# Masking attention's future keys: zeroed in the exponentials on VectorE, or added to the scores on TensorE

## The reference, cut to what matters

```python
scores = jnp.einsum('bhqd,bhkd->bhqk', q, k) / math.sqrt(hd)
causal = jnp.triu(jnp.ones((S, S), dtype=bool), k=1)
scores = jnp.where(causal[None, None], -jnp.inf, scores)
attn = jax.nn.softmax(scores, axis=-1)
attn_out = jnp.einsum('bhqk,bhkd->bhqd', attn, v)
```

## Time and profile before

| | us |
|---|---|
| median of 3 runs | 1922.88 (1922.86 to 1925.65) |
| the profiled execution | 1917.86 |
| its span, first to last instruction | 1916.0 |
| TensorE busy | 1823.9 (95%) |
| VectorE busy | 1022.4 (53%) |
| ScalarE busy | 744.5 (39%) |
| GpSimd busy | 659.2 (34%) |

### The profile page before, as it was taken

The page is one execution under the profiler, slowest core; times in us unless marked ns, Lnnn a source line. Parts: engine busy times, 40 slices in busy tenths (PEclk is TensorE's granted clock), DMA queues, the critical chain, the costliest instruction groups (busy, mean ns, idle before and its releaser), DMA issues.

```text
span 1916.0 us, 29823 instructions
## 1 busy us (share of the span) xinstructions
PE 1823.9 (95%) x11604; PEld 1361.1 (71%) x11604; DVE 1022.4 (53%) x2155; ACT 744.5 (39%) x1542; POOL 659.2 (34%) x831
## 2 busy tenths in 40 slices
PE   4886899999999999999999999999999999999888
PEld 2575746986489845997479855997479864898457
DVE  5675365635565365645655365644656365653531
ACT  5842345133542346133452245223451335322441
POOL 2242333423353233523343232632343232532110
PEclk9897999999999999999999999999999999999789
DMA  4001000000000000000000000000000000000000
GB/s 151 11 23 45 12 2 11 1 1 23 12 1 1 12 12 12 1 1 23 12 1 1 11 13 12 1 1 22 12 1 1 1 23 1 1 1 11 1 1 11
DMA packets 20202, 23.78 MB, mean 12 GB/s; under 512 B 960, under 2 KB 18784, under 8 KB 20064
## 3 DMA queue, kind: packets, MB, share of 16 engines
q1 hardware_dynamic: 19728, 20.83, 3.4%
q0 software_dynamic: 336, 1.05, 0.2%
HBM read 17.68 MB, written 4.19 MB: 11 GB/s over the span
## 4 chain that ended last, share of the span: by engine, by line
PE 84%; DVE 4%; ACT 2%; issue 2%; POOL 1%; POOLq 0%; DVEq 0%; ACTq 0%
PE ring L1457 17%; PE ring L1442 17%; PE ring L1497 8%; PE ring L1418 7%; PE ring L1428 6%; PE ring L1594 5%; PE attn_out L1614 4%; PE ring L1552 3%; PE ring L1574 3%; PE ring L1577 2%; PE ring L1410 2%; PE ring L1597 2%; PE ring L1466 2%; PE ring L1528 1%; PE ring L1530 1%
## 5 line engine op out<-in xcount | busy, mean ns | idle before, releaser
L1203 DVE TENSOR_REDUCE maxes<-ring 128x2 f32<-128x768 f32 (+7 forms) x292 | 198.0, 735 | 91.8 <-PE ring L1577 90.9
L1127 DVE COPY_PREDICATED scores_t<-masks,ring 128x512 f32<-128x512 uint16 x224 | 160.7, 731 | 104.2 <-issue 95.3
L670 POOL TENSOR_TENSOR rstd<-mean_var,eps_and_power 128x2 f32<-128x2 f32 x96 | 19.3, 201 | 493.1 <-DVE mean_var L1050 493.1
L1497 PEld LDWEIGHTS ring<-big 128*128 128x128 f32 x1536 | 180.4, 194 | 10.8 <-issue 4.9
L1497 PE MATMUL ring<-big 128*128 128x128 f32 x1536 | 182.7, 277 | 4.4 <-POOL big L721 3.1
L721 POOL TENSOR_TENSOR big<-big,decay_blocks 128x256 f32<-128x256 f32 x192 | 141.0, 747 | 111.3 <-issue 86.5
L1457 PE MATMUL ring<-w_down,big 128*128 128x256 f32 x768 | 172.4, 380 | 0.0
L1457 PEld LDWEIGHTS ring<-w_down,big 128*128 128x128 f32 x768 | 144.5, 190 | 18.5
L693 POOL TENSOR_TENSOR mix<-mix,z_t 128x512 f32<-128x512 f32 x80 | 86.2, 1104 | 152.4 <-DVE mix L1097 152.4
L1594 PE MATMUL ring<-big 32*128 32x512 f32 (+3 forms) x1024 | 123.9, 481 | 3.4 <-issue 1.7
L894 ACT ACTIVATE big<-ring,up_bias 128x256 f32<-128x256 f32 x192 | 80.5, 470 | 99.0 <-PE ring L1442 99.0
(11 more groups left out here) (192 smaller groups left out, 3483.2 us busy)
## 6 DMA issues: line engine op xcount, KB each, us to landing
x_in<-in_x SPq DMA_DIRECT2D x8, 512.0 KB, 3.8
out<-x_z_xb SPq DMA_DIRECT2D x8, 512.0 KB, 2.9
delta<-in_x SPq DMA_DIRECT2D x7, 512.0 KB, 3.8
w_mlp<-in_wm SPq DMA_DIRECT2D x2, 1024.0 KB, 7.0
w_mlp<-in_w_exp_t SPq DMA_DIRECT2D x1, 1028.0 KB, 14.1
v_ones<-in_w_con SPq DMA_DIRECT2D x1, 1024.0 KB, 9.9
w_k<-in_wk SPq DMA_DIRECT2D x1, 512.0 KB, 7.4
rope<-in_rope POOLq DMA_DIRECT2D x1, 512.0 KB, 6.6
```

Source lines behind the costliest of these rows:

```text
L1127: ins = nc.vector.copy_predicated(scores[:, h, :, :], lmask[:, lv, :].bitcast(U16).unsqueeze(1) .to_broadcast([P, NT, P]), chunks)
L1203: nc.vector.tensor_reduce(maxes[:, t % 2, qt, 32 * gs[0] + row:32 * gs[-1] + row + 1:32], banks[:, first:last, lo:hi], AX_X, ALU.max).then ...
L1497: ins = mm(ps[:, tok], kg[:, h, tok], q[:, h, tok], start=True, stop=True)
```

## The change

The mask product of `s_exp` goes. The score products are no longer followed by an accumulating product, so each carries its own stop flag, and the last part's product signals that the bank is full. A new step `hide(t, rnd)`, only on VectorE, waits until the four exponentials of the round are written and then overwrites with zero those that belong to future keys, with one predicated copy of 128x512 (4 heads x 128 queries) in rounds a and c and two in round b. Its mask is the tile `future_t` read as 16-bit words; its data is one zero element, broadcast. `V(t, rnd)` waits for `hide(t, rnd)` in place of the four exponentials. The list places hide(t,a) behind S(t+1,a), hide(t,b) behind S(t+1,b) and hide(t,c) behind S(t+1,c). The masks of S stay.

```diff
@@ attention_steps
-        o += fill[0] + [("E", t, "b")] + fill[1] + [("V", t, "a")]
+        o += [("hide", t, "a")] + fill[0] + [("E", t, "b")] + fill[1] + [("V", t, "a")]
         o += [("S", t + 1, "b")] if ahead else []
+        o += [("hide", t, "b")]
         o += [("roundq", 3, "all")] if t == 1 else []
         o += [("V", t, "b")] + fill[2] + [("E", t, "c")] if ahead else fill[2] + [("E", t, "c"), ("V", t, "b")]
         o += [("S", t + 1, "c")] if ahead else []
-        o += fill[3] + [("V", t, "c")]
+        o += [("hide", t, "c")] + fill[3] + [("V", t, "c")]
@@ VectorE
+            def future_hidden(t, part):
+                dve.wait_ge(*after(pt_ready, exp_count(t, part, HG - 1)))
+                if b == 0 and t == 0 and part == "a":
+                    dve.wait_ge(*loaded(masks_in))
+                    dve.wait_ge(consts.h, N_CONSTS)
+                for at in (0, P) if part == "b" else (0,):
+                    ins = nc.vector.copy_predicated(pt[part][:, :, at:at + P], future_t.bitcast(U16).unsqueeze(1)
+                                                    .to_broadcast([P, HG, P]),
+                                                    zt[:, 0, 0:1].unsqueeze(1).to_broadcast([P, HG, P]))
+                ins.then_inc(*one(hidden_ready))
@@ s_exp
-                        mm(ps[g][:, at:at + n], kp[r, t, jt * P:(jt + 1) * P], qp[r, t, jt * P:T],
-                           start=(i == 0), stop=False)
-                for g in range(HG):
-                    mm(ps[g][:, 0:hi], identb, future_t.unsqueeze(1).to_broadcast([P, hi // P, P]),
-                       start=False, stop=True).then_inc(*filled(("E", t, rnd, g)))
+                        ins = mm(ps[g][:, at:at + n], kp[r, t, jt * P:(jt + 1) * P], qp[r, t, jt * P:T],
+                                 start=True, stop=True)
+                        if i == len(parts) - 1:
+                            ins.then_inc(*filled(("E", t, rnd, g)))
@@ pv
+                pe.wait_ge(*after(hidden_ready, used_count(t, rnd)))
                 for jt, lo in {"a": ((0, 0),), "b": ((1, P), (3, 0)), "c": ((2, 0),)}[rnd]:
                     n = T - jt * P
                     for g in range(HG):
                         m = NH // 2 * jt + HG * (t // 2) + g
-                        pe.wait_ge(*after(pt_ready, exp_count(t, rnd, g)))
```

More of the change, by code:

```diff
@@ L432, in hybrid_kernel @@
         pt_ready = sem("p_ready", NH * 3)
+        hidden_ready = sem("future_hidden", 3 * NG)
         pt_used = sem("p_used", 3 * NG)
@@ L1368, in _ @@
                     shift(*at)
+                elif kind == "hide":
+                    future_hidden(*at)
                 elif kind == "divide":
@@ L1585, in s_exp @@
                 parts = {"a": ((0, 0),), "b": ((1, P), (3, 0)), "c": ((2, 0),)}[rnd]
-                hi = 2 * P if rnd == "b" else P
                 ps = []
```

## The result

The changed kernel takes 2101.9 us (2099.7 to 2104.8, 4 runs) against 1922.9 us of the kernel before, a ratio of 1.0931 (95% interval 1.0910 to 1.0953): 179 us slower. The prediction was 2088 us. The profiled execution took 2103.3 us with a span of 2101.5.

What follows compares the result with a forecast made beforehand. TensorE, busy 95% of the span, was taken as the bound. Waits net of saved masks (94 us) plus lower clock (71 us) added 165 us to 1922.9, giving 2088 us; range 2005 to 2165.

Steps and rivals of the forecast that it cites:

- The long waits: V(t,b) in groups 0 to 2 waits for maxima and hides: 4.0, 4.1 and 3.9 us, 12.0 us a batch.
- The small waits: Shorter waits for hides before V(2,a), V(3,a), V(2,c), V(3,c), V(1,c) and V(3,b): 4.9 us a batch in sum.
- rival 2: Hides blocked by GpSimd's SBUF reads (10 us), or low clock through whole groups: 2138 us; above 2125, chance 0.14.
- The masks: 384 mask products leave TensorE, saving 1.20 us a group, 4.7 us a batch, 37.6 us if nothing else moved.
- The waits inside E(t,c): While TensorE waits, banks come free and waits inside E(t,c) vanish: 0.8 us a batch taken off.
- The clock: Long waits drop TensorE's granted clock, 3.2 us a fall: 9.6 us a batch, 71 us in all.
- The sum: Whole kernel: 94 us for waits and masks plus 71 us for the clock, 165 us slower, 2088 us.
- The last batch: No products cover V(t,c) there: some 3 us more of waits, and about 4 us for the clock.
- Rival 1: The waits come, but TensorE's clock holds or recovers inside the wait: 2017 us; 2000 to 2050, chance 0.18.
- Rival 3: Hides fit under other work and only the saved mask products remain: 1885 us; chance 0.04.
- Rival 4: The change doesn't do what it says: mask words not seen as true, or hides overlap something; no time of its own.

Runs made afterwards that it cites:

- experiment 5: Changed kernel with hide(t,b) placed ahead of the row maxima of S(t+1,b) in VectorE's queue; 2021.0 us, ratio 1.0535 to the kernel before.
- experiment 3: Changed kernel with 16 zero products on TensorE ahead of each wait of V(t,b), t = 0 to 2; 2031.3 us, ratio 1.0615 to the kernel before.
- experiment 1: Changed kernel without any hide, so neither mask products in E nor zeroing, future keys left unmasked; 1910.0 us, ratio 0.9958 to the kernel before.
- experiment 4: Kernel before, masks kept and no hides, with V(t,b), t = 0 to 2, waiting for the row maxima of S(t+1,b); 2024.3 us, ratio 1.0558.
- experiment 6: Kernel of experiment 5 with GpSimd's sums of the mixes replaced by zero fills that only write; 1982.5 us, ratio 1.0330 to the kernel before.
- experiment 2: Kernel of experiment 1 with three zero products ahead of wa's wait in batches 1 to 7; 1908.1 us, ratio 0.9948 to the kernel before.
- experiment 8: Kernel before with zero products where TensorE waits, in the last batch only; 1906.9 us, ratio 0.9941 to the kernel before.

## Why the prediction was right

**The long waits: right.** 4.0, 4.1 and 3.9 us were forecast, 3.76, 3.67 and 3.67 measured, 11.1 against 12.0 a batch. The mechanism is shown by experiment 5, where a change of order alone takes part of them away. The pair of hides costs 1.33 us, where 1.38 was taken.

**The small waits: right in number, a little smaller in sum.** V(2,a) 1.29 (1.1), V(3,a) 1.20 (1.2), V(3,c) 1.10 (0.9); V(2,c) is none in the changed kernel and 1.05 us with the clock up (1.2). Sum 3.6, and 4.65 with the clock up (experiment 3), where 4.9 was taken ahead of the correction for the low clock. V(2,a) holds part of rival 2: its hide takes 1.28 us in place of 0.73, beside GpSimd's division, 0.55 us a batch against the 0.6 of that rival. The other half of it didn't come: hide(0,c) takes 0.73 us, and GpSimd's rounding beside it 1.00 in place of 0.62.

**The masks: mis-sized, and the step that failed.** That a group saves 1.20 us and "a batch 4.7 us" is true of what the products occupy on TensorE and not of the time: experiment 1 gives 8 us in all, 1 us a batch, and 2.4 us in a batch without a fall. The prediction itself had said that an instruction taken from TensorE is worth its full length only where its queue is gapless; the queue was gapless because the masks stood in it. The waits inside E(t,c) did vanish as forecast: in experiment 3 E(1,c) and E(2,c) take 0.71 us each, in the kernel before 1.23 and 0.99. But others came in, which the sum put at nothing: by TensorE's idle time other than for hides (18.5 - 14.7 = 3.8 us against 1.2) 2.6 us a batch.

**The clock: right in mechanism, near in size.** 9.6 us a steady batch were forecast, 10.4 measured by experiment 3. That it comes so near is in part luck: the prediction has three falls at 3.2 us, the changed kernel four a batch, which makes 2.6 us each. In experiment 4, with waits of 2.5 us, a fall costs 1.7. That the longer waits of the changed kernel leave the clock low for longer is what the two clocks say (0.83 against 0.91), four falls against three included. The fourth comes behind the wait of 1.18 us near 1243 us, and the prediction had placed it in group 3. That each wait of 2.4 us or more brings a fall, as its rows had it, holds for 19 of 21 in experiment 4.

**The sum.** For a steady batch 21.0 us were forecast and 23.2 came in batch 4. Waits and masks without the clock were to be 11.4 us and are 12.8 by experiment 3: +2.6 for the waits that the masks had covered, -0.9 for the long waits, -0.3 for the small ones. The clock adds 0.8. The last batch was forecast at 18 us and grew by 25.3: its idle time by 18.8, where 12.0 + 4.9 - 0.8 + 3 = 19.1 were taken, and its busy time by 6.5, where -4.7 for the masks and 4 for the clock were. So the clock's 4 us is what was too small there: with the masks' 4.7 gone it is some 11 (an estimate, 6.5 + 4.7). By the traces 2083 us were forecast and 2103.3 came, 14 us of the difference from the seven batches and 7 from the last. A slip in the range: three pairs 0.6 us shorter in 8 batches are 14 us, not 12, which nothing hangs on.

**The rivals.** Rival 1, the clock holds: out, by experiment 3 and by the clock of 0.83. Rival 3, the hides fit under other work: out, as VectorE's timeline shows. Rival 4 has nothing for it: the mask products are gone and the copies are there in their number. Rival 2's blocking is real (experiment 6), but small in this order of the queue, as only one hide a batch is lengthened by it there.

What stays open: what decides whether a wait of about 1 or 2.5 us brings a fall, and where the falls without a wait come from; and how the masks' saving would look if each wait that came in for them were removed as well, which wasn't tried.

## What to carry to other kernels

Before an instruction is taken from the bounding engine, look at what the other engines do in the time that it covers: a gapless queue doesn't say that each piece of it is worth its length. Before a step is put between two engines, look at the receiving engine's queue at the moment when the result is wanted; its busy share says nothing of it (53% here, and a wait of 3.7 us at three places a batch). Count a wait on TensorE of 2.4 us or more as the wait and, nearly every time here, a slow stretch behind it of 1.7 to 2.6 us. Where falls come and go from batch to batch, read all batches and not one.

## What the runs showed of the hardware

- A wait of TensorE can be had at less cost if it does something: 16 zero products in the place of a 3.7 us wait kept the granted clock at 1.00 and saved 10.4 us a batch; 12 us were won so in the last batch of the kernel before alone.
- Which waits bring a fall isn't to be told from their length alone: 1.18 us ahead of one product did in batch 4 of experiment 2, and 1.19 at the same place in experiment 1 did not, where a fall had come earlier. In batches 0 to 6 waits of 2.4 to 2.8 us did in 19 of 21 cases (experiment 4), waits of 2.45 in 5 of 7 (experiment 6), waits of 3.6 to 3.9 in 21 of 21 (the changed kernel). Once a fall came with no wait just ahead of it (experiment 8, batch 2), for 1.6 us.
- A pair of COPY_PREDICATED of 128x512 with mask and data in SBUF takes 1.33 us alone, 2.38 us beside one GpSimd sum and 3.07 us beside three and a rounding; beside GpSimd fills and the start of a rounding 1.33, and then the rounding takes 1.15 us in place of 0.62.
